# The first chunk of a DLRM interaction tower taken through its start in two halves of 16 examples

## What is computed

```python
prev = x
for k in range(3):
    z = jnp.einsum('bmd,bhd->bdmh', x, prev).reshape(b, D, m * h)
    t = jnp.einsum('bdc,co->bdo', z, ws[k]) + bs[k]
    t = jnp.transpose(t, (0, 2, 1))
    t = t / jnp.sqrt(jnp.sum(t * t, axis=(-2, -1), keepdims=True))
    logit.append(t); prev = t
h = concat(sum(concat(logit), axis=-1), dense_ctx)      # (512, 384 + 16)
y = relu(relu(h @ W_top1 + b_top1) @ W_top2 + b_top2) @ W_top3
```

## Time and profile before

| | us |
|---|---|
| time, median of 3 runs (1111.45 to 1113.16) | 1112.04 |
| time of the profiled execution | 1112.11 |
| its span | 1110.4 |
| first matmul of layer 1 starts | 51.36 |

### The profile page before, as it was taken

How to read it: one execution, slowest core, us unless ns; L and a number is a source line. 1 busy time by engine, 2 the same in 40 slices (tenths; PEclk the granted TensorE clock), 3 DMA queues, 4 the chain that set the end, 5 groups by cost and what they waited for, 6 DMA issues and landing times.

```text
span 1110.4 us, 17904 instructions
## 1 busy us (share of the span) xinstructions
PE 1054.2 (95%) x4394; PEld 790.2 (71%) x4394; DVE 939.3 (85%) x3189; ACT 814.9 (73%) x2756; POOL 902.5 (81%) x726
## 2 busy tenths in 40 slices
PE   0798999999999999999999999999999999999999
PEld 0366677777777777777777777777777777778773
DVE  2476899898999989899989989998998988898892
ACT  3366686877778687777878787787878777788872
POOL 5687898888989898888888888898888888577760
PEclk9898999999999999999999999999999999999999
DMA  6503040210303011020303002020300203000000
GB/s 228 127 13 72 3 122 3 43 32 3 72 3 72 3 43 32 6 69 3 73 3 67 8 10 66 3 72 3 73 2 14 61 4 72 0 1 1 1 1 1
DMA packets 56735, 41.20 MB, mean 37 GB/s; under 512 B 37915, under 2 KB 40859, under 8 KB 56502
## 3 DMA queue, kind: packets, MB, share of 16 engines
q1 hardware_dynamic: 49145, 32.17, 12.5%
q10 hardware_dynamic: 2365, 6.60, 1.7%
q0 software_dynamic: 5120, 1.29, 1.3%
HBM read 38.09 MB, written 1.94 MB: 36 GB/s over the span
## 4 chain that ended last, share of the span: by engine, by line
PE 59%; POOL 26%; ACT 7%; issue 5%; DMA 2%; DVE 1%; SPq 0%; POOLq 0%; ACTq 0%; DVEq 0%
POOL sums L329 21%; PE acc L615 9%; PE bank_a L550 9%; PE bank_a L552 8%; PE bank_a L551 8%; PE bank_d L550 7%; PE bank_d L552 7%; PE bank_d L551 7%; POOL gathered L317 5%; ACT scaled L437 5%; ACT t L461 1%; PE turned L591 1%; PE bank_a L680 1%; ACT squares L464 1%; PE bank_d L704 1%
## 5 line engine op out<-in xcount | busy, mean ns | idle before, releaser
L329 POOL TENSOR_TENSOR sums<-sums,scaled 128x512 f32<-128x512 f32 x512 | 686.5, 1342 | 132.3 <-ACT scaled L437 97.5
L752 DVE SCALAR_TENSOR_TENSOR sums<-bank_d,x_col,sums 128x128 f32<-128x128 f32 x2176 | 627.3, 339 | 102.7 <-PE bank_d L552 68.4
L437 ACT ACTIVATE scaled<-bank_a,x_col 128x128 f32<-128x128 f32 x2048 | 586.0, 382 | 150.9 <-PE bank_a L552 144.8
L550 PE MATMUL bank_a<-w_hi,prev_lo 128*128 128x512 f32 x640 | 282.2, 441 | 20.5 <-ACT scaled L437 9.2
L550 PE MATMUL bank_d<-w_hi,prev_lo 128*128 128x512 f32 (+1 forms) x640 | 277.2, 433 | 1.1 <-DVE sums L771 1.1
L552 PE MATMUL bank_a<-w_hi,prev_hi 128*128 128x512 f32 x640 | 253.4, 396 | 0.0
L551 PE MATMUL bank_a<-w_lo,prev_hi 128*128 128x512 f32 x640 | 252.9, 395 | 0.0
L552 PE MATMUL bank_d<-w_hi,prev_hi 128*128 128x512 f32 (+1 forms) x640 | 245.4, 383 | 0.0
L551 PE MATMUL bank_d<-w_lo,prev_hi 128*128 128x512 f32 (+1 forms) x640 | 245.2, 383 | 0.0
L317 POOL DMA_INDIRECT gathered<-in_table,idx x160 | 169.3, 1058 | 31.1 <-issue 19.7
L437 ACT ACTIVATE sums<-bank_a,x_col 128x128 f32<-128x128 f32 x512 | 146.7, 373 | 63.2 <-PE bank_a L552 63.2
(11 more groups left out here) (59 smaller groups left out, 484.2 us busy)
## 6 DMA issues: line engine op xcount, KB each, us to landing
x_pairs<-x_scratch SPq DMA_DIRECT2D x141, 156.0 KB
x_pairs<-x_scratch SPq DMA_DIRECT2D x78, 78.0 KB
gathered<-in_table,idx POOLq DMA_INDIRECT x160
w_raw<-in_w ACTq DMA_DIRECT2D x2, 768.0 KB, 6.7
x_scratch<-gathered SPq DMA_DIRECT2D x16, 72.0 KB
w_raw<-in_w ACTq DMA_DIRECT2D x1, 1024.0 KB, 5.2
w_raw<-in_w ACTq DMA_DIRECT2D x1, 896.0 KB
w_raw<-in_w ACTq DMA_DIRECT2D x1, 832.0 KB
```

What stands on the lines that cost most here:

```text
L329: nc.gpsimd.tensor_tensor(out=sums[:, n % SUMS, :, :], in0=sums[:, n % SUMS, :, :], in1=scaled[:, a - 1, :, :], op=ALU.add).then_inc(a_add ...
L437: op = nc.scalar.activation(to[:, i, :], bank_a[at % A_RING][:, i * UNITS:(i + 1) * UNITS], ACT.Copy, scale=x_of(c, q, a * PER_BANK + i))
L550: nc.tensor.matmul(to, lo, w_h, start=True, stop=False)
L752: nc.vector.scalar_tensor_tensor(out=taken(n, u) if u in LEFT else total, in0=taken(n, u), scalar=x_of(c, q, A_FIELDS + u), in1=total, op0 ...
```

## The change

Chunk 0 becomes two halves of 16 examples; the second is called `OTHER_HALF` (-1). Each half has its own 5 gathers, its own scratch, 3 store DMAs and 14 load DMAs of half the width (1 KB rows where 2 KB were), its own pairs, layer-0 sums (the second half's in the bank `turned`), `finish`, norm, `make_prev`, `high`, `low` and `turn_x`. ACT issues the loads of w0 and the biases first, waits for the ids, and then issues w1 and two thirds of w2; the last third follows after `copy_x(0)`. All of chunk 0's load DMAs are issued by SP; before, ACT issued p1 and p3. Chunk 1's gathers are cut by `low(1, 0)` after the seventh, and of chunk 2's gathers two stand in the lead, where three stood ahead of it. Half 0 is `c = 0` and `turn_of(OTHER_HALF)` is 1.

```diff
@@ POOL
-            for j in range(GATHERS):
+            for j in range(HALF_GATHERS):
                 gather(0, j)
             nc.gpsimd.memset(ones[:, :], 1.0).then_inc(ones_made, 1)
             ...
+            for j in range(HALF_GATHERS, GATHERS):
+                gather(0, j)
             start_chunk(1)
             for j in range(GATHERS):
+                if j == LOW_BEFORE:
+                    low(1, 0)
                 gather(1, j)
             start_chunk(2)
-            for j in range(GATHERS_BEFORE):
-                gather(2, j)
-            low(1, 0)
             for at in range(LEAD):
                 add_bank(at)
+                if at == 2:
+                    low(1, OTHER_HALF)
+                if at >= LEAD - GATHERS_BEFORE:
+                    gather(2, at - LEAD + GATHERS_BEFORE)
@@ SP
-            store_chunk(0)
-            for c in range(CHUNKS):
-                sp.wait_ge(scratch_stored, (c + 1) * 48)
-                if c:
-                    sp.wait_ge(pairs_made, c * NP)
-                    sp.wait_ge(x_turn_done, c)
-                for p in range(NP) if c else SP_GROUPS:
+            for half, c in enumerate((0, OTHER_HALF)):
+                store_half(half)
+                sp.wait_ge(half_stored, (half + 1) * 48)
+                for p in range(NP):
+                    load_pairs(sp, c, p)
+            store_chunk(1)
+            for c in range(1, CHUNKS):
+                sp.wait_ge(scratch_stored, c * 48)
+                sp.wait_ge(pairs_made, turn_of(c) * NP)
+                sp.wait_ge(x_turn_done, turn_of(c))
+                for p in range(NP):
                     load_pairs(sp, c, p)
@@ ACT
-            load_raw(1)
             act.dma_start(w0_sb[0:PAIR_ROWS, :, :], w0a).then_inc(w0_loaded, 16)
             ...
-            load_raw(2)
+            act.wait_ge(ids_loaded, 32)
+            for part in range(len(W_LOADS[1])):
+                load_raw(1, part)
+            for part in range(W2_LOADS_FIRST):
+                load_raw(2, part)
             ...
             copy_x(0)
+            for part in range(W2_LOADS_FIRST, len(W_LOADS[2])):
+                load_raw(2, part)
             finish(0, 0)
+            split_high(2, W2_FIRST)
             roots(0)
             high(1, 0)
+            finish(0, OTHER_HALF)
+            split_high(2, W2_FIRST + 1)
             for at in range(LEAD):
                 scale_bank(at)
+                if at == 1:
+                    roots(1)
+                if at == 3:
+                    high(1, OTHER_HALF)
+                if at == LEAD - 1:
+                    copy_x(OTHER_HALF)
@@ PE
-            keep_busy(3)
+            keep_busy(2)
             turn_x(0)
             pe.wait_ge(w0_folded, 2)
             for tile in range(PAIR_TILES):
                 pair_matmul(0, tile)
-            keep_busy(2)
+            for tile in range(3):
+                pair_matmul(OTHER_HALF, tile)
             norms(0)
-            keep_busy(4)
+            for tile in range(3, PAIR_TILES):
+                pair_matmul(OTHER_HALF, tile)
+            keep_busy(1)
             for at in range(LEAD):
                 bank_for_act(at)
+                if at == 1:
+                    norms(1)
+            turn_x(OTHER_HALF)
@@ DVE
-            for p in range(NP):
-                make_pairs(0, p)
-            for piece in range(W2_FIRST, W2_SECOND):
-                split_low(2, piece)
-            sum_values(0, 0)
-            sum_squares(0, 0)
-            ...
-            dve.wait_ge(prev_lo_made[1], 1)
-            for piece in range(W2_SECOND, len(W_PIECES[2])):
+            for c in (0, OTHER_HALF):
+                for p in range(NP):
+                    make_pairs(c, p)
+            norm_steps(0, 0)
+            norm_steps(1, OTHER_HALF)
+            for piece in range(W2_FIRST, W2_FIRST + 2):
                 split_low(2, piece)
+                    if (n, u) == (0, 18):
+                        split_low(2, W2_FIRST + 2)
```

More of the change, by code:

```diff
@@ L17 @@
 SLOT_FIELDS = 128 // CB
+HALF_CB = CB // 2
+HALF_GATHERS = GATHERS // 2
+HALF_FIELDS = 128 // HALF_CB
+HALF_LAST_SLOTS = FIELDS * HALF_CB - (HALF_GATHERS - 1) * 128
+HALF_SCRATCH_FIELDS = FIELDS + 3 * HALF_FIELDS
+OTHER_HALF = -1
 LAST_SLOTS = FIELDS * CB - (GATHERS - 1) * 128
@@ L97 @@
     for _k, _c in _items:
-        if _at and _k < 2:
+        if _at and _k < 2 and _c != OTHER_HALF:
             if _c == (1 if _k == 0 else 0):
@@ L258, in cin_kernel, with turn_of, chunk_of, examples_of @@
         R_STEPS = 4
+        def turn_of(c):
+            return 1 if c == OTHER_HALF else c + (c > 0)
+        def chunk_of(c):
+            return max(c, 0)
+        def examples_of(k, c):
+            if k or c > 0:
+                return slice(0, CB)
+            return slice(0, HALF_CB) if c == 0 else slice(HALF_CB, CB)
+        def columns_of(k, c):
+            b = examples_of(k, c)
+            return slice(b.start * EMB, b.stop * EMB)
+        def inputs_made(k, c):
+            return turn_of(c) + 1 if k == 1 else c + 1
+        def gathered_by(c):
+            return 16 * (HALF_GATHERS + GATHERS * c)
         def d_fields_of(d):
@@ L270, in load_pairs @@
         def load_pairs(queue, c, p):
-            rows = scratch[c, :, :].rearrange("(m b) e -> m (b e)", b=CB)
+            if c > 0:
+                rows = scratch[c, :, :].rearrange("(m b) e -> m (b e)", b=CB)
+            else:
+                rows = scratch_half[turn_of(c), :, :].rearrange("(m b) e -> m (b e)", b=HALF_CB)
+            at_columns = columns_of(0, c)
+            width = at_columns.stop - at_columns.start
+            landed = half_loaded[p] if c == 0 else pairs_loaded[p]
             tiles = PAIR_GROUPS[p]
@@ L276, in load_pairs @@
                 if p == 0:
-                    queue.dma_start(x_rep[at, :], rows[0:FIELDS, :]).then_inc(pairs_loaded[p], 16)
+                    queue.dma_start(x_rep[at, at_columns], rows[0:FIELDS, :]).then_inc(landed, 16)
                 offsets = [PAIR_OFFSETS[PER_TILE * i + kk] for i in tiles if PER_TILE * i + kk < OFFSETS]
@@ L281, in load_pairs, with wait_pairs_loaded @@
                     window = bass.AP(first.tensor, first.offset,
-                                     [[ROWS, FIELDS], [PER_TILE * ROWS, len(offsets)], [1, ROWS]])
-                    queue.dma_start(x_rot[at, tiles[0]:tiles[0] + len(offsets), :],
-                                    window).then_inc(pairs_loaded[p], 16)
+                                     [[width, FIELDS], [PER_TILE * width, len(offsets)], [1, width]])
+                    queue.dma_start(x_rot[at, tiles[0]:tiles[0] + len(offsets), at_columns],
+                                    window).then_inc(landed, 16)
+        def wait_pairs_loaded(engine, c, p):
+            if c == 0:
+                engine.wait_ge(half_loaded[p], PAIR_LOADS[p] * 16)
+            else:
+                engine.wait_ge(pairs_loaded[p], turn_of(c) * PAIR_LOADS[p] * 16)
         def bdim(ap):
@@ L587, in turn_sums @@
                 pe.wait_ge(merged, MERGES * (n + 1))
-                if q == 0 and n >= TILES:
-                    k, c, _ = JOBS[n - 1]
+                if q == 0:
+                    k, c, _ = JOBS[n - 1] if n else (0, OTHER_HALF, 0)
                     pe.wait_ge(squared, FINISH_NO[k, c] + 1)
@@ L601, in turn_x @@
                 begun["turns"] += 1
-                for q in range(TILES):
+                at = columns_of(0, c)
+                for q in range(at.start // COLS, at.stop // COLS):
                     op = nc.tensor.transpose(x_turned[:, q * (FIELDS + 1):(q + 1) * (FIELDS + 1)],
@@ L912 @@
     arrays = {
-        "ids": slots(np.asarray(inputs["ids"])),
-        "bases": lay(slots(np.broadcast_to(starts, (BATCH, FIELDS)))[:, 0:GATHERS]),
+        "ids": both(np.asarray(inputs["ids"])),
+        "bases": lay(both(np.broadcast_to(starts, (BATCH, FIELDS)))[:, 0:2 * GATHERS].reshape(128, 2, GATHERS)),
         "table": lay(np.concatenate(tables, axis=0)),
```

206 lines of the change are left out of this document (127 added, 79 removed).

## The result

The change made the kernel slightly slower. After: median 1115.53 us (1114.65 to 1116.91, 9 runs); before, beside it: 1112.78 (1111.45 to 1114.17, 9 runs); ratio 1.0027, 95% interval 1.0017 to 1.0037. The prediction was 1106.5, range 1101 to 1111. The profiled execution took 1114.89 us, 2.78 more than the one of before.

What follows compares the result with a forecast made beforehand. PE, busy 95% of the span, was taken as the bound from job 0 on. The profiled 1112.1 us minus 6.0 at chunk 1 plus 0.5 at chunk 2 gave 1106.6, median 1106.5, range 1101 to 1111.

Steps and rivals of the forecast that it cites:

- The start: Ids, gathers, stores and loads of chunk 0's halves up to the first norm, claimed to start at 37.5 against 45.35.
- Layer 1 at 44.41, not 42.3: Norm to layer 1: first matmul claimed at 42.3, 9.1 us sooner, between 41.3 at full clock and 44.0 at 0.50.
- The three signs named for being wrong: Half 1's stores far from 26.8, PE holding layer 1 back over 2 us, or job 2's wait growing.
- PE sums them at 57.6 where it did at 63.61: 6.0 sooner: Chunk 1's first pair sums: three of layer 1's nine us go to late loads, 6.0 us of gain remain.
- the wait of 2.8: At chunk 1's first pairs DVE is ready at 52.9 but p0 lands at 55.7, so it waits 2.8 us.
- 0.43 us for each us at 1.2 GHz: Rate from matmul counts behind job 2's wait: each us PE spends at granted clock 0.50 costs 0.43 us.
- keeps its 4.07: PE's wait for `low(1, 1)` in job 2 stays 4.07 us, as does the 5.2 us at clock 0.50 behind it.
- 0.8 of wait, of which I count 0.5: Chunk 2's last gather moves back 2.4 us, giving 0.8 us of wait, 0.5 added to the sum.
- the slack of 1.6: Chunk 2 in the kernel before: p0 landed near 100.9 and was wanted at 102.47, 1.6 us to spare.
- The rival with the right sign: Slower: PE stays at clock 0.50 for 18 us through the lead and job 0, 1114 us; chance 0.06.
- The rival of loads that cost by the row: Each half's loads take 10.4 us to land, not 7.3, so half 1 comes 3.1 later, 1110.2 us; chance 0.13.

Runs made afterwards that it cites:

- a_fill: Changed kernel plus matmuls nobody reads in PE's waits for chunk 1's and chunk 2's data, no transfer moved; 1112.30 us, ratio to before 0.9990.
- a_low_last: Changed kernel with all ten gathers of chunk 1 ahead of `low(1, 0)`; 1115.11 us, ratio to before 1.0023.
- l_more: Changed kernel, POOL's order alone changed: chunk 1's ten gathers and three of chunk 2 ahead of `low(1, 0)`, four behind; 1104.79 us, ratio to before 0.9922.
- b_more: Kernel before with six gathers of chunk 2 ahead of the lead, four before `low(1, 0)` and two behind; 1108.05 us, ratio 0.9942.
- b_gather2: Kernel before with only chunk 2's gathers placed as late as in the change, two in the lead; 1116.13 us, ratio 1.0019.
- c_fill: Changed kernel with early column turn, POOL's order of before, unread matmuls in job 2's wait and between the halves; 1108.81 us, ratio to before 0.9955.
- b_ids_fill: Kernel before with w1 and w2 loaded after the ids, plus three unread matmuls in job 2's wait; 1114.16 us, ratio 1.0003.
- d_more: Changed kernel, early column turn, chunk 1's ten gathers and three of chunk 2 before `low(1, 0)`, four behind; 1102.25 us, ratio to before 0.9902.
- a_gather3: Changed kernel with three of chunk 2's gathers in the lead, its last one place earlier; 1108.99 us, ratio to before 0.9967.
- b_ids_first: Kernel before with only the load order changed: w0 and biases first, w1 and w2 after the ids; 1111.97 us, ratio 0.9987.

## Why the prediction was wrong

**The start, right to 2 us.** The index add began at 5.33 (5.4 said); half 0's loads began at 19.75 (20.0), half 1's stores at 25.72, which is when SP had issued half 0's loads (25.7 was named as its bound, 26.8 taken), its loads at 30.89 (29.8), `dsum` at 38.83 (37.5). Half 1's gathers were slow as said (3.13 for the first). The store took 5.2 instead of 3.0.

**Layer 1 at 44.41, not 42.3.** Of these 2.1, 1.3 are `dsum`'s own lateness. For the rest, the prediction gave 41.3 at full clock and 44.0 at 0.50 and took a value nearer the first; half 1's last tiles took 3.76 for four, with the granted clock at 0.50 from 40.0 to 43.6.

The three signs named for being wrong all stayed away: half 1's stores were 1.1 from 26.8, PE held layer 1 for 1.3 us behind `prev_lo` (43.09), and job 2's wait shrank. They looked at the start, and the loss came behind it.

**The step that failed first: "PE sums them at 57.6 where it did at 63.61: 6.0 sooner".** It was 61.81, 1.8 sooner. Of the 4.2 missing, 2.2 are layer 1's own lateness, carried through the seven banks and the turn (loads at 52.83, not 50.6), 1.1 are p0's landing (6.2 after the first load issue, not 5.1), 0.8 the products (2.59, not 1.8). The landing was read off the queue's bytes: in 4.8 us SP's queue had moved 0.75 MB here and 0.76 before, more than p0's 0.72, but part of that belonged to later groups. And then the sum stopped: it took the wait of 2.8 as the whole price. Behind the wait PE ran 7.6 us at a mean clock of 0.58 and lost another 3.1, so that the turn of job 0 was 1.3 late instead of 6.0 early. The prediction had the rate for this, 0.43 us for each us at 1.2 GHz, and used it for a rival with 18 us of low clock only; it didn't apply it to the new waits of its own forecast. a_fill, with the clock full, is 2.6 faster from layer 1's start to that turn, so most of the 3.1 is the low clock's. How much low clock follows a wait isn't fixed: a_low_last with like waits lost 1.6 less there.

**Job 2's wait: "keeps its 4.07", ending near 83.** It fell to 2.19 and ended at 88.62. Beside before, PE came 1.3 later to it and POOL's `low(1, 1)` 0.6 sooner (87.31 for 87.87), not some 6 as the forecast had it. In after that was a gain of 2.8, the clock behind it included; l_more and b_more show that all of the wait could go.

**Chunk 2: "0.8 of wait, of which I count 0.5".** It was 2.3 and its clock, 4.1 together. The last gather came 1.9 later than before (2.4 said), and p0 landed at 103.47, 1.0 behind the time at which before asked for it (0.8 said). But the slack of 1.6 was reckoned with job 2's wait unchanged; with this shorter, DVE asked 1.4 sooner than before, at 101.09, and waited 2.4. b_gather2 shows that the late gather costs the kernel before as well, and a_low_last, c_fill and b_ids_fill that what is won ahead of it is waited away.

**The sum by its parts.** Predicted -5.5, profiled +2.8, 8.3 off: 7.3 at chunk 1 (4.2 of stations, 3.1 of clock), 2.8 won back at job 2, 3.6 more than counted at chunk 2, 1.6 of low clock behind the wait for `low(2, 0)`, which the sum didn't have and which is not the change's, and -1.4 spread behind it.

**The rival with the right sign had the wrong mechanism.** Low clock through the lead and job 0, 1114, at 0.06: PE was at 1.2 GHz in half 1's tiles, but its mean clock from 44.4 to 58 was 1.00; the low clock came behind the waits. The rival of loads that cost by the row says that half of the new loads are of 40 KB; it is 10 of 28. What should have been a rival of weight is that chunk 2's gather, on an engine that the change loads further, takes all of it back.

**What halving is worth.** With neither transfer late, d_more against b_more: 0.9902 to 0.9942, some 4.4 us, 4.1 in the table at job 0. l_more against b_more is 0.3 at job 0: with the turn of half 1 behind the lead, chunk 1's wait eats the halves' lead whole. These pairs also differ by one gather's place and by all else in the change, the order of the loads above all, so this is the worth of the whole change and not of the halves alone.

## What to carry to other kernels

Follow an earlier start through the next two refills (here chunk 1's and chunk 2's transfers), not the next one; each has its own slack, and the first that is short caps the gain whatever comes before it. Price each new wait of TensorE with the slow stretch behind it, here 1.6 to 3.1 us on waits of 2 to 4, and in some executions nothing. Before moving the work of the bound engine, look for holes in the engine that feeds it: POOL's 6 to 9 us of idling before the lead, filled with gathers that were due later, were worth 6.5 us without the change and 10.7 with it, by the medians. When a profile names no releaser, look at which semaphore the program waits for at that matmul, and at what ended just before it.

## What the runs showed of the hardware

- TensorE's granted clock fell to 0.50 (1.2 GHz) behind idle stretches of 2.0 to 2.3 us as behind one of 4.1, and wait and slow stretch together cost 4.1 us where the wait was 2.32, and 6.2 where it was 4.07. It is not certain and not fixed: behind the 2.0 us wait for `low(2, 0)` it fell in 15 traces and not in 3, behind job 2's wait it stayed full in a_gather3 (2.24) and a_low_last (2.23), and b_ids_first's wait of 4.14 cost 5.3.
- One gather issued while DVE split weights held POOL for 3.13 us, and the four behind it 1.29, 1.23, 1.70 and, when the splits had ended, 0.93. In the whole trace of after, the 111 gathers that no weight split and no product of pairs on DVE overlaps took 0.91 to 1.11 us; of the 49 that one overlaps, 18 took 1.2 to 3.1. The Trainium skill (SBUF — State Buffer, Who interferes with whom) infers that DVE's two-input instructions don't stall descriptor generation; these rows speak against it, as the earlier trace rows did, though no run takes the splits away.
- Loads of half the width: half 1's 14 were issued from 30.89 and the last products could start at 37.89, 7.0 later (7.3 expected by bytes, 10.4 by rows). Chunk 1's 14 of full width took 10.8 from the first issue to the last packet, so half the bytes took about two thirds of the time. Half 0's, beside the weights' transfers, took from 19.75 to 29.91, 10.2.
